# Two groups of eight tiles or four chains of four in a matrix normalisation, and a fourth weight pair in high and low parts

## The chip, the cores and the metric

The kernel runs on one core of one Trainium2 chip. The metric is the time of one execution on the device in microseconds (us), the median of three runs. An engine is named as in the profile: PE is the matrix engine (PEld its weight loads), DVE the vector engine, ACT the scalar engine, POOL the GpSimd engine, SP the engine that issues most DMA transfers (SPq its queue).

## The reference, cut to what matters

Eight samples of 256 tokens, 1024 features, float32. Each sample chooses one of 16 dense weights and one of 8 low-rank adapters. Cut to what is computed:

```python
# part one
h = einsum('bij,bkj->bik', x, L0_weight[ids1])      # a 1024 x 1024 weight per sample
h = layernorm(h) * gamma + beta
h = quant(h) @ quant(w1).T + b1                     # int8 fake-quant, scale per row
h = gelu(h)
h = quant(h) @ quant(w3).T + b3
x1 = x + h
# part two
c = x1 @ base_w.T + bias + scale * (x1 @ A[ids2].T) @ B[ids2].T
n = c / rms(c)
Hres = sinkhorn_log(n @ W_res.T + base)             # 4 x 4 per token, 50 iterations
Hpre, Hpost = softmax(n @ W_pre.T + ..), softmax(n @ W_post.T + ..)
Hres = (1 - g) * I + g * Hres                       # g = sigmoid(gate)
s = c as 4 streams of 256
out = x1 + Hres @ s + Hpost * ((Hpre . s) @ W_branch)
```

## The kernel before, in words

The tokens are 16 tiles of 128, two to a sample. The order of each engine's instructions is written out by hand: every engine has its own program (`step_a`, `step_b` and a tail, one version of each per engine), and semaphores tie them together. Nothing is reordered, so what waits on an engine holds up all that is written behind it.

**Part one** (0 to 398 us) has a `step_a(s)` for each sample s. PE's order in one is: transposes and product with w3 for the tiles of sample s-2, the transposes and product with w1 for sample s-1, and between them the four pairs `l0(s, 0..3)` of the gathered weight, a pair being two of the eight 128-row pieces. The products are L1087, the transposes L1019. A pair is computed in one of two ways. As it was loaded (L1010, `w_raw` times `x_raw`, float32), or in parts (L998): ACT rounds weight and x to high parts in the type fp32r (L731, L732), DVE subtracts these from the values to get low parts (L1546 for x, L1547 for the weight), and PE does high times high, low times high, and high times low. `parted(s, pr)` says which pairs are done so: pairs 0 to 2 of samples 3 to 6 (`FIRST = 3`). The high and low halves have no buffers of their own: `w_high(pr)` lies in `w_lo[pr]`, the x parts in `w_lo[3]`, and the four `w_hi` and `w_lo` are free until the base weight of part two is split into them (`split_hi`, ACT L616; low parts by DVE), which happens in the steps of samples 6 and 7. The work between two products of one tile is: ACT evacuates `hbuf` (L633), takes the sum of squares (L642), DVE centres and scales it, ACT rounds it (L652), PE transposes it, ACT evacuates `qT` (L672); after w1 DVE scales (L1461), ACT does the gelu (L657) and rounds again (L661, `quant2`); after w3 DVE writes `x1buf` (L1488).

In the same stretch rows for part two are prepared: the low parts of the adapter rows and of the heads' rows, written to the scratch tensor `stack_low_scratch` by SP. Four stores count `all_st` up to 64: two in the step of sample 2, two (`store_head_rows`, L358 and L359) in that of sample 6 (`step_a_base`). `heads_in` and `bias_in`, from which the last two go, lie in the memory of the `w_hi` buffers. So ACT waits for `all_st` before `split_hi(3)`.

**Part two** (398 to 621 us) has a `step_b(b)` per sample: base weight in high and low parts (L1204, three quarters of the step), the adapter, the heads, the softmaxes, the branch input. A product of the adapter or the heads is L1192; it stands once a step on the chain. In steps 0 to 3 DVE has idle stretches ahead of `xT_lo` (L1539), the low part of the transposed tiles.

**The Sinkhorn normalisation** is done on the factors: DVE alternates row and column factors `ka`, `kb`, each by a product (L1725), a sum (L1729) and a reciprocal (L1732); 49 iterations run in this loop, and the start (L1691 to L1716, `sinkhorn_start`) and the finish (L1746 to L1755) do the rest. The 16 tiles are two groups of 8, and each group two chains of 4 tiles whose instructions alternate, 12 an iteration. Group 0 is started after step 3, and its iterations stand in the steps of samples 4 to 7 as 11, 12, 13 and 13 (`B_ITERS`); group 1 is started after the last softmax, and all its iterations follow it.

**The tail** (621 to 749 us): while DVE iterates group 1, ACT and PE mix the first eight tiles. For one tile ACT builds `post` (L927, four instructions) and `blk` (L935, sixteen) from the 4 x 4 matrices, PE adds the rest and the branch (L1310, L1316) and `blk` times the streams (L1325), and ACT evacuates (L942). `select(g)` (L1339) and `pick(g)` (DVE L1787, L1794) bring the matrices of a group into the form `hs` that the blocks need. The rest and branch of the last eight tiles are done there too, ahead of their matrices (`AHEAD = 4` of them first, four at the end), and then PE has only `blk` times streams left (L1356), with blocks by DVE (L1821) and three by ACT (`BY_ACT`), and DVE adds (L1835). Before it `keep_warm` runs 48 transposes (L1366) while the last three iterations go on.

## Time and profile before

| | |
|---|---|
| median of three runs | 749.83 us (749.0, 749.83, 750.52) |
| the profiled execution, its own time | 751.13 us |
| its span, first to last instruction | 749.3 us |
| PE busy | 707.8 us, 94% |
| DVE busy | 526.2 us, 70% |
| ACT busy | 397.3 us, 53% |
| POOL busy | 79.9 us, 11% |
| mean granted clock of PE | 0.977 of full |
| chain of waits, share by engine | PE 74%, DVE 19%, ACT 5%, issue 2%, DMA 1% |

The span in 40 slices of 18.7 us. A digit is the busy share in tenths, 9 for 90% or more; PEclk is the clock granted to PE:

```profile
PE   8999999999999999999998999999999993999957
DVE  4569676979742976776663341428899998999985
ACT  1255846666741584828355443444534432899614
PEclk9999999999999999999998999999999996999979
```

PE is the bound until about 717 us; then DVE alone works until the last factors are there, and after it PE and DVE finish the last eight tiles.

### The profile page before, as it was taken

The page shows a single profiled execution, that of the slowest core. Times are in us where ns is not written, and L with a number is a line of the kernel's source. Part 1 is how long each engine was busy: PE and PEld are TensorE (multiplying, and loading weights), DVE is VectorE, ACT ScalarE, POOL GpSimd, SP SyncE. Part 2 cuts the span into 40 slices and gives each one's busy share as a digit, 9 for nine tenths or more (in the row PEclk, how much of TensorE's full clock was granted, in tenths as well). Part 3 has the DMA queues.
Part 4 walks back from the last instruction along what each step waited for, and adds up shares of the span by engine and source line. Part 5 has one row for each costly group of instructions (what it writes and reads, how often), then busy time and mean ns, then how long its engine had stood idle before and what let it go on. Part 6 is the DMA issues. An engine that isn't in the chain of part 4 may idle for free.

```text
span 749.3 us, 10394 instructions
## 1 busy us (share of the span) xinstructions
PE 707.8 (94%) x3292; PEld 477.6 (64%) x3292; DVE 526.2 (70%) x1869; ACT 397.3 (53%) x714; POOL 79.9 (11%) x57
## 2 busy tenths in 40 slices
PE   8999999999999999999998999999999993999957
PEld 5444445656536565445656888887888872677656
DVE  4569676979742976776663341428899998999985
ACT  1255846666741584828355443444534432899614
POOL 0201400302030032732040000000000000000000
PEclk9999999999999999999998999999999996999979
DMA  7997255558734236851232303303123086847106
GB/s 297 409 410 284 94 196 207 187 165 300 294 111 169 101 126 197 327 199 64 69 127 74 127 13 115 127 0 128 56 74 128 0 281 224 262 162 244 64 1 224
DMA packets 52477, 124.35 MB, mean 166 GB/s; under 512 B 6211, under 2 KB 31939, under 8 KB 46920
## 3 DMA queue, kind: packets, MB, share of 16 engines
q1 hardware_dynamic: 51128, 120.96, 45.6%
q10 hardware_dynamic: 1296, 2.74, 1.0%
q8 instruction: 26, 0.43, 0.2%
q14 instruction: 27, 0.22, 0.1%
HBM read 97.96 MB, written 25.72 MB: 165 GB/s over the span
## 4 chain that ended last, share of the span: by engine, by line
PE 74%; DVE 19%; ACT 5%; issue 2%; DMA 1%; SPq 0%; ACTq 0%; DVEq 0%
PE PS L1204 20%; PE PS L1010 18%; PE PS L1087 13%; PE PS L998 8%; DVE kprod L1725 4%; DVE ksum L1729 4%; PE PS L1192 2%; PE PS L1019 2%; DVE ka L1732 2%; DVE kb L1732 2%; PE PS L1356 2%; PE PS L1121 2%; PE PS L1178 2%; PE PS L1238 1%; PE PS L1366 1%
## 5 line engine op out<-in xcount | busy, mean ns | idle before, releaser
L1010 PE MATMUL PS<-w_raw,x_raw 128*128 128x512 f32 x320 | 141.7, 596 | 1.3 <-DMA w_raw<-cond_w_dram 0.9
L1010 PEld LDWEIGHTS PS<-w_raw,x_raw 128*128 128x128 f32 x320 | 59.4, 190 | 69.6 <-issue 69.6
L1204 PE MATMUL PS<-w_hi,xT_hi 128*128 128x512 f32 x256 | 103.0, 402 | 0.0
L1204 PE MATMUL PS<-w_hi,xT_lo 128*128 128x512 f32 x256 | 100.5, 393 | 0.0
L1204 PE MATMUL PS<-w_lo,xT_hi 128*128 128x512 f32 x256 | 100.4, 392 | 0.0
L1539 DVE TENSOR_TENSOR xT_lo<-PS,xT_hi 128x512 fp32r<-128x512 f32 x32 | 20.5, 682 | 66.0 <-ACT xT_hi L753 66.0
L1729 DVE TENSOR_REDUCE ksum<-kprod 128x16 f32<-128x64 f32 x392 | 66.3, 211 | 0.0
L577 POOL TENSOR_TENSOR xres<-xres,vecs 128x1024 f32<-128x1024 f32 x16 | 42.5, 2680 | 218.1 <-DMA xres<-x_tok_dram 218.1
L672 ACT ACTIVATE qT<-PS,round_c 128x1024 bf16<-128x1024 f16 x32 | 35.4, 1108 | 56.6 <-PE PS L1019 56.6
L1087 PE MATMUL PS<-w3q,qT 128*128 128x512 bf16 x256 | 57.8, 379 | 1.0 <-ACT qT L672 1.0
L1087 PE MATMUL PS<-w1q,qT 128*128 128x512 bf16 x256 | 57.9, 379 | 0.3 <-ACT qT L672 0.3
L1204 PEld LDWEIGHTS PS<-w_hi,xT_lo 128*128 128x128 f32 x256 | 48.3, 189 | 10.4
L1204 PEld LDWEIGHTS PS<-w_lo,xT_hi 128*128 128x128 f32 x256 | 48.5, 190 | 9.2
L1204 PEld LDWEIGHTS PS<-w_hi,xT_hi 128*128 128x128 f32 x256 | 48.6, 190 | 9.1
L833 ACT ACTIVATE y<-PS 128x512 f32<-128x512 f32 x32 | 18.0, 592 | 57.0 <-PE PS L1212 57.0
L1087 PEld LDWEIGHTS PS<-w1q,qT 128*128 128x128 bf16 x256 | 24.5, 98 | 32.6 <-issue 5.5
L1087 PEld LDWEIGHTS PS<-w3q,qT 128*128 128x128 bf16 x256 | 24.2, 98 | 33.2 <-issue 4.4
L1461 DVE SCALAR_TENSOR_TENSOR gbuf<-PS,lnst,vecs 128x512 f32<-128x512 f32 x32 | 23.5, 748 | 30.9 <-PE PS L1087 30.8
L998 PE MATMUL PS<-w_lo 128*128 128x512 f32 x96 | 38.6, 402 | 1.2 <-DVE w_low L1547 1.0
L998 PE MATMUL PS<-w_lo,x_low 128*128 128x512 f32 x96 | 38.0, 395 | 0.0
L998 PE MATMUL PS<-w_low,w_lo 128*128 128x512 f32 x96 | 37.8, 394 | 0.0
L1488 DVE SCALAR_TENSOR_TENSOR x1buf<-PS,q2st,vecs 128x512 f32<-128x512 f32 x32 | 23.0, 746 | 19.1 <-PE PS L1087 19.1
(209 smaller groups left out, 1358.0 us busy)
## 6 DMA issues: line engine op xcount, KB each, us to landing
w_raw<-cond_w_dram SPq DMA_DIRECT2D x31, 1024.0 KB, 5.4
x_raw<-x_tr_dram SPq DMA_DIRECT2D x32, 256.0 KB, 6.7
stage<-w_dram SPq DMA_DIRECT2D x16, 512.0 KB, 16.2
xres<-x_tok_dram SPq DMA_DIRECT2D x8, 1024.0 KB, 8.2
x_scratch<-x1buf SPq DMA_DIRECT2D x16, 512.0 KB, 6.7
x1n<-x_scratch SPq DMA_DIRECT2D x16, 512.0 KB, 6.6
y_scratch<-y SPq DMA_DIRECT2D x16, 512.0 KB, 3.7
stage<-base_w_nat_dram SPq DMA_DIRECT2D x8, 512.0 KB, 8.7
```

Of the source, the lines that this page charges most:

```text
L577: nc.gpsimd.tensor_tensor(xres[:, t, :], xres[:, t, :], vecs[:, V_B3, :], ALU.add).then_inc(xb3_done, 1)
L672: nc.scalar.activation(qT[t][:, :, :], PS[:, T_BANK + t, :].bitcast(F16).rearrange("p (c n) -> p c n", c=KC), ACT.Identity, bias=round_c[: ...
L998: mm = pe.matmul(PS[:, 2 * t + h, :], xx[:, c, t * P:(t + 1) * P], ws[:, c, h * H2:(h + 1) * H2], start=(pr == 0 and c == 0 and xx is xh a ...
L1010: mm = pe.matmul(PS[:, 2 * t + h, :], x_raw[pr][:, c, t * P:(t + 1) * P], w_raw[pr][:, c, h * H2:(h + 1) * H2], start=(pr == 0 and c == 0) ...
L1087: mm = pe.matmul(PS[:, O_BANK + h, :], qT[t][:, c, :], wq[:, c, h * H2:(h + 1) * H2], start=(c == 0), stop=(c == KC - 1))
L1204: pe.matmul(PS[:, 2 * t + h, :], xx[:, c, t * P:(t + 1) * P], ws[c // 2][:, c % 2, h * H2:(h + 1) * H2], start=(c == 0 and xx is xT_hi and ...
L1461: nc.vector.scalar_tensor_tensor(out=g[:, h * H2:(h + 1) * H2], in0=PS[:, O_BANK + h, :], scalar=lnst[:, t, 8:9], in1=vecs[:, V_SW1, h * H ...
L1488: nc.vector.scalar_tensor_tensor(out=x1buf[t][:, h * H2:(h + 1) * H2], in0=PS[:, O_BANK + h, :], scalar=q2st[:, t, 1:2], in1=vecs[:, V_SW3 ...
L1539: nc.vector.tensor_tensor(xT_lo[:, 4 * h:4 * h + 4, t * P:(t + 1) * P], PS[:, T_BANK + h, :].rearrange("p (c n) -> p c n", c=4), xT_hi[:, ...
L1725: nc.vector.tensor_tensor(kprod[i][:, :, :, :], (kmat if row else kmat_t)[i][:, :, :, :], cols(v, HG), ALU.mult).then_inc(k_step[i], 1)
L1729: nc.vector.tensor_reduce(ksum[i][:, :, :], kprod[i][:, :, :, :], AX.X, ALU.add).then_inc(k_step[i], 1)
L1732: nc.vector.reciprocal(new[i][:, :, :], ksum[i][:, :, :]).then_inc(k_step[i], 1)
```

## The change

Of part one:

- Pair 3 is also done in parts, for samples 4, 5 and 6 (`FIRST = (3, 3, 3, 4)`). Its high weight part goes to `w_hi[3]`. ACT rounds it ahead of pairs 0 and 1 of the next sample, DVE takes its low part in the same place.
- `heads_in` and `bias_in` lie two places lower (`2 * PAIRS - 4`), in the memory of `w_hi[2]`. So ACT's wait for `all_st` stands before `split_hi(2)`, and SP issues `store_head_rows` one transfer earlier, ahead of `load_base(3)`.
- Two transfers `load_nat(6)` and `load_nat(7)` of the step of sample 4 go behind the loads of weight pair 3. The semaphores `ln_mean` and `ln_var` are one, `ln_stat`.

Of part two and the tail:

- The Sinkhorn work is four chains of four tiles. `sinkhorn_start` does one chain, in steps 2, 4 and 6 and after the last softmax. The shares of iterations per step are in `SHARES`: chain 0 alone in steps 2 and 3, chains 0 and 1 together in 4 and 5, four iterations of them and the finish of chain 0 in step 6, then chains 1 and 2.
- After the last softmax: chain 3 is started; 6 iterations of chains 1 and 3, finish of 1, 33 iterations of chains 2 and 3 (with `pick_first` after two and `lo_xp` after eight), finish of 2, then chain 3 alone: 3 iterations, `pick(2)`, 1, two mixing blocks, 6, finish.
- Twelve tiles are mixed as eight were before (`MIXED`), the blocks of the last two of these by DVE; four tiles are left for the end (`LAST`), one of their blocks by ACT. `AHEAD` is 2, `BLK` 5. `select` and `pick` come in three: for tiles 0 to 7, 8 to 11 and 12 to 15. `keep_warm` runs 24 transposes during the last two iterations.
- The finish of a chain uses the product that the loop left in `kprod` for the last column factor; the one that was made anew is gone.

The first place: SP's queue in the step of sample 6, before and after. `w_raw<-cond_w_dram` is the load of sample 7's weight pair 1, which waits until DVE has read the buffer.

Before:

```order
L314 TENSOR_LOAD ids
L314 ISA x2
L320 ISA [waits wlo_done]
L320 DMA w_raw<-cond_w_dram 128x2048
L310 DMA x_raw<-x_tr_dram 128x512
L325 DMA w_raw<-base_w_dram 128x2048 [waits l0_pair]
L358 DMA stack_low_scratch<-heads_in 128x24 [waits all_low]
L359 DMA stack_low_scratch<-bias_in 1x24
```
After, the same stretch:

```order
L327 TENSOR_LOAD ids
L327 ISA x2
L333 ISA [waits wlo_done]
L333 DMA w_raw<-cond_w_dram 128x2048
L323 DMA x_raw<-x_tr_dram 128x512
L371 DMA stack_low_scratch<-heads_in 128x24 [waits all_low]
L372 DMA stack_low_scratch<-bias_in 1x24
L338 DMA w_raw<-base_w_dram 128x2048 [waits l0_pair]
```
The two stores now stand one transfer earlier, ahead of the base weight's piece 3, and still behind the weight load that waits for `wlo_done`.

The second place: ACT in the steps of samples 6 and 7, with the semaphores an instruction waits for. L616 and L631 are `split_hi`; the first one shown is `split_hi(2)`. What follows it is the gelu (L657, L672) and quant2 (L661, L676) of tile 1 of sample 5.

Before:

```order
L642 ACTIVATE x1buf,lnst<-hbuf,lnst 128x1024 [waits x1_st0,ln_mean]
L616 ACTIVATE w_hi<-w_raw 128x2048 [waits wld2]
L657 ACTIVATE gbuf<-gbuf 128x1024 [waits g_pre]
L648 ACT_TABLE_LOAD
L648 ACTIVATE lnst<-lnst 128x1 [waits ln_step]
L661 ACTIVATE gbuf<-gbuf,round_c,q2st 128x1024 [waits g_step]
L639 ACTIVATE lnst<-lnst 128x1 [waits l0_evac]
L642 ACTIVATE x1buf,lnst<-hbuf,lnst 128x1024 [waits x1_st1,ln_mean]
L652 ACTIVATE hbuf<-hbuf,round_c,lnst 128x1024 [waits ln_step]
L672 ACTIVATE qT<-PS,round_c 128x1024 [waits t3_done,m1_done]
L616 ACTIVATE w_hi<-w_raw 128x2048 [waits all_st,wld3]
```
After:

```order
L657 ACTIVATE x1buf,lnst<-hbuf,lnst 128x1024 [waits x1_st0,ln_stat]
L631 ACTIVATE w_hi<-w_raw 128x2048 [waits all_st,wld2]
L672 ACTIVATE gbuf<-gbuf 128x1024 [waits g_pre]
L663 ACT_TABLE_LOAD
L663 ACTIVATE lnst<-lnst 128x1 [waits ln_step]
L676 ACTIVATE gbuf<-gbuf,round_c,q2st 128x1024 [waits g_step]
L654 ACTIVATE lnst<-lnst 128x1 [waits l0_evac]
L657 ACTIVATE x1buf,lnst<-hbuf,lnst 128x1024 [waits x1_st1,ln_stat]
L667 ACTIVATE hbuf<-hbuf,round_c,lnst 128x1024 [waits ln_step]
L687 ACTIVATE qT<-PS,round_c 128x1024 [waits t3_done,m1_done]
L631 ACTIVATE w_hi<-w_raw 128x2048 [waits wld3]
```
The wait for `all_st` has moved nine instructions up, from the split of piece 3 to that of piece 2, so that the gelu and quant2 of that tile now stand behind it.

The third place: DVE in the step of sample 5, with buffer numbers. `x1buf1` is the end of sample 3's tile 1, `gbuf0` the scaling after w1 of sample 4's tile 0.

Before:

```order
L1493 TENSOR_TENSOR x1buf1<-x1buf1,xres 128x1024
L1546 TENSOR_TENSOR x_low0<-x_raw0,w_lo3 128x512
L1547 TENSOR_TENSOR w_low0<-w_raw0,w_lo0 128x2048
L1546 TENSOR_TENSOR x_low1<-x_raw1,w_lo3 128x512
L1547 TENSOR_TENSOR w_low1<-w_raw1,w_lo1 128x2048
L1461 SCALAR_TENSOR_TENSOR gbuf0<-PS,lnst,vecs 128x512 x2
L1465 TENSOR_TENSOR gbuf0<-gbuf0,vecs 128x1024
```
After:

```order
L1542 TENSOR_TENSOR x1buf1<-x1buf1,xres 128x1024
L1595 TENSOR_TENSOR x_low3<-x_raw3,w_lo3 128x512
L1596 TENSOR_TENSOR w_low3<-w_raw3,w_hi3 128x2048
L1595 TENSOR_TENSOR x_low0<-x_raw0,w_lo3 128x512
L1596 TENSOR_TENSOR w_low0<-w_raw0,w_lo0 128x2048
L1595 TENSOR_TENSOR x_low1<-x_raw1,w_lo3 128x512
L1596 TENSOR_TENSOR w_low1<-w_raw1,w_lo1 128x2048
L1510 SCALAR_TENSOR_TENSOR gbuf0<-PS,lnst,vecs 128x512 x2
```
One more pair of low parts stands ahead of the two that were there, and `gbuf0` behind all three.

The fourth place: the end of PE's program. L1310 and L1335 add the rest, L1316 and L1341 the branch, L1325 and L1353 the mixing, L1339 and L1379 are `select`, L1366 and L1406 `keep_warm`.

Before, from the mixing of tile 7 on, up to the first of the last eight tiles:

```order
L1325 MATMUL PS<-my3,blk1 128x256 x4
L1310 MATMUL PS<-nr4,ident 128x512 x2
L1316 MATMUL PS<-br,post0 128x256 x4
L1310 MATMUL PS<-nr5,ident 128x512 x2
L1316 MATMUL PS<-br,post1 128x256 x4
L1310 MATMUL PS<-nr6,ident 128x512 x2
L1316 MATMUL PS<-br,post0 128x256 x4
L1310 MATMUL PS<-nr7,ident 128x512 x2
L1316 MATMUL PS<-br,post1 128x256 x4
L1366 MATMUL PS<-ident 128x128 x48
L1339 MATMUL PS<-hres1,sel 128x128 x4
L1356 MATMUL PS<-ny0,my0 128x256 x4
```
After, the same end begins:

```order
L1335 MATMUL PS<-nr2,ident 128x512 x2
L1341 MATMUL PS<-br,post0 128x256 x4
L1335 MATMUL PS<-nr3,ident 128x512 x2
L1341 MATMUL PS<-br,post1 128x256 x4
L1379 MATMUL PS<-hres1,sel 128x64 x4
L1335 MATMUL PS<-mr0,ident 128x512 x2
L1341 MATMUL PS<-br,post0 128x256 x4
L1353 MATMUL PS<-my0,blk3 128x256 x4
```
and ends:

```order
L1335 MATMUL PS<-mr3,ident 128x512 x2
L1341 MATMUL PS<-br,post1 128x256 x4
L1353 MATMUL PS<-my3,blk1 128x256 x4
L1406 MATMUL PS<-ident 128x128 x24
L1379 MATMUL PS<-hres1,sel 128x64 x4
L1396 MATMUL PS<-ny0,my0 128x256 x4
```
Four tiles that PE mixed after the last select now go before it, behind a select of their own, and two rest-only tiles are behind the eighth instead of four.

The diff, cut to its core:

```diff
-    FIRST = 3
+    FIRST = (3, 3, 3, 4)
-    BLK = 3
-    BY_ACT = (5, 6, 7)
-    AHEAD = 4
+    BLK = 5
+    CHAINS = NT // HG
+    LAST = HG
+    MIXED = NT - LAST
+    BY_ACT = (LAST - 1,)
+    BY_DVE = (MIXED - 2, MIXED - 1)
+    AHEAD = 2
...
         def parted(s, pr):
-            return FIRST <= s < GUEST and pr < PAIRS - 1
+            return FIRST[pr] <= s < GUEST
...
         def w_high(pr):
-            return w_lo[pr]
+            return w_hi[pr] if pr == PAIRS - 1 else w_lo[pr]
...
-        B_ITERS = (11, 12, 13, 13)
-        WARM_ITERS, WARM_LAST = 3, 48
+        STARTS = {2: 0, 4: 1, 6: 2}
+        SHARES = {2: (2, 3, 3, 3), 3: (3, 3, 2, 3), 4: (2, 3, 3, 3), 5: (3, 3, 3, 3), 7: (3, 3, 4, 0)}
+        FIRST_REST, SECOND_SHARES = 4, (3, 3)
+        WARM_ITERS, WARM_LAST = 2, 24
...
                 load_w(s + 1, 1)
+                store_head_rows()
                 load_base(3)
-                store_head_rows()
...
             def split_hi(pr):
                 act.wait_ge(wld[pr], pair_loads(GUEST - 1, pr) + 16)
-                if pr == PAIRS - 1:
+                if pr == PAIRS - 2:
                     act.wait_ge(all_st, 64)
...
                 evac_T(s - 1, 0, 1)
+                if s < GUEST:
+                    pair_high(s, 3)
                 pair_high(s + 1, 0)
...
                 finish_w3(s - 2, 1)
+                if s < GUEST:
+                    pair_low(s, 3)
                 pair_low(s + 1, 0)
...
             def step_b(b, first=False, last=False):
                 def share(i):
+                    if b in SHARES:
+                        iterations(SHARES[b][i], *((0,) if b < 4 else (0, 1) if b < 6 else (1, 2)))
+                    elif b == NB - 2 and i == 0:
+                        iterations(FIRST_REST, 0, 1)
+                        sinkhorn_finish(0)
+                    elif b == NB - 2 and i >= 2:
+                        iterations(SECOND_SHARES[i - 2], 1, 2)
                 lo_stacks(b)
                 if not first:
                     lo_xp(b - 1)
+                if b in STARTS:
+                    sinkhorn_start(STARTS[b], nothing)
                 share(0)
...
-            sinkhorn_start(1)
+            sinkhorn_start(3, beside_last_start)
             gather_next(NB - 1, 3)
-            iterations(1, 0, 2)
-            pick(0)
-            iterations(1, 2, 8)
+            iterations(SINKHORN - 1 - done[1], 1, 3)
+            sinkhorn_finish(1)
+            iterations(2, 2, 3)
+            pick_first()
+            iterations(6, 2, 3)
             lo_xp(NB - 1)
-            iterations(1, 10, SINKHORN - 11)
-            sinkhorn_finish(1)
+            iterations(SINKHORN - 1 - done[2], 2, 3)
+            sinkhorn_finish(2)
+            iterations(3, 3)
+            pick(2)
+            iterations(1, 3)
+            dve.wait_ge(hs_step, 4)
+            for k in BY_DVE:
+                mix_block(k)
+            iterations(SINKHORN - 1 - done[3], 3)
+            sinkhorn_finish(3)
...
-            select(0)
-            for i in range(AHEAD):
...
+            rest_only(0, 0)
+            branch_transposes(NB - 1)
+            rest_only(1, 1)
+            select_first()
+            mix(0)
+            branch(NB - 1)
+            for k in range(1, GROUP):
+                mix(k)
+            rest_only(AHEAD + GROUP, 2)
+            rest_only(AHEAD + GROUP + 1, 3)
+            select(2)
+            for k in range(GROUP, MIXED):
+                mix(k)
             keep_warm()
-            select(1)
-            for i in range(GROUP):
+            select(3)
+            for i in range(LAST):
                 last(i)
```

## Rows read from the trace of the kernel before

**Rows 1.** The chain of waits, steps 3 to 7: start, length, piece.
```profile
475.95 2.87 PE PS L1192 x24
...
537.47 2.87 PE PS L1192 x24
...
567.41 2.87 PE PS L1192 x24
...
578.08 5.48 PE PS L1204 x24
...
609.41 5.48 PE PS L1204 x24
```

**Rows 2.** The chain of waits, the last eight tiles.
```profile
728.65 14.05 PE PS L1356 x56
```

**Rows 3.** The chain of waits, steps of samples 3 to 5.
```profile
166.96 5.61 PE PS L998 x24
...
195.53 6.92 PE PS L1010 x16
```

**Rows 4.** Timeline of ACT, step of sample 6: start, length, instruction, [idle, releaser].
```profile
307.17 1.90 ACT L616 ACTIVATE w_hi<-w_raw 128x2048 fp32r<-128x2048 f32 x1
...
311.69 1.24 ACT L661 ACTIVATE gbuf<-gbuf,round_c,q2st 128x1024 f32<-128x1024 f32 x1 [0.16 <-DVE q2st L1476]
```

**Rows 5.** Timeline of DVE, step of sample 5.
```profile
254.49 0.69 DVE L1546 TENSOR_TENSOR x_low<-x_raw,w_lo 128x512 fp32r<-128x512 f32 x1
...
257.29 1.40 DVE L1461 SCALAR_TENSOR_TENSOR gbuf<-PS,lnst,vecs 128x512 f32<-128x512 f32 x2
```

**Rows 6.** Timeline of PE, steps of samples 6 and 7.
```profile
265.10 0.47 PE L998 MATMUL PS<-w_lo 128*128 128x512 f32 x1 [0.22 <-ACT hbuf L633]
...
314.90 0.61 PE L1019 MATMUL PS<-ident,gbuf 128*128 128x128 f16 x8
```

**Rows 7.** Timeline of SP's queue, the store of the bias row of the heads.
```profile
309.58 0.32 SPq L359 DMA_DIRECT2D stack_low_scratch<-bias_in  x1
```

**Rows 8.** The tile stack_low_scratch: all its DMAs, from issue to landing.
```profile
DMA to landing us min/median/max: 2.2/3.5/3.8
```

**Rows 9.** Timeline of DVE, steps of samples 3 and 4.
```profile
494.07 1.29 DVE L1539 TENSOR_TENSOR xT_lo<-PS,xT_hi 128x512 fp32r<-128x512 f32 x2 [12.85 <-ACT xT_hi L753]
...
508.95 0.29 DVE L1691 TENSOR_REDUCE ska<-zall 128x32 f32<-128x128 f32 x1
...
514.60 0.09 DVE L1716 MEMSET kb<- 128x16 f32 x2
```

**Rows 10.** Timeline of DVE, from the last softmax to the last factor.
```profile
623.34 0.17 DVE L1595 TENSOR_SCALAR hd<-hd 128x2 f32<-128x2 f32 x1 [1.13 <-ACT sq L837]
...
634.23 0.28 DVE L1691 TENSOR_REDUCE ska<-zall 128x32 f32<-128x128 f32 x1
...
640.85 0.35 DVE L1725 TENSOR_TENSOR kprod<-kmat,kb 128x64 f32<-128x64 f32 x2
...
644.10 0.69 DVE L1787 TENSOR_TENSOR hsr<-PS,mask_r 128x256 f32<-128x256 f32 x2
...
723.00 0.29 DVE L1753 TENSOR_SCALAR hres<-hres,gate_c 128x128 f32<-128x128 f32 x1
723.33 0.26 DVE L1755 TENSOR_SCALAR hres<-hres,gate_c 128x32 f32<-128x32 f32 x1
```

**Rows 11.** Timeline of ACT, one tile of the mixing.
```profile
672.75 1.40 ACT L927 ACTIVATE post<-ident,hp 128x128 f32<-128x128 f32 x4
673.93 3.51 ACT L935 ACTIVATE blk<-mask,hs 128x32 f32<-128x32 f32 x16
```

**Rows 12.** Busy time by stretch: us, busy us (instructions) of each engine, PEclk granted.
```profile
650.00:694.00 44.00, 42.87 (x170) 30.96 (x169) 44.00 (x323) 44.00 (x170) 0.00 (x0) 1.00 0.68 221
...
717.00:719.00 2.00, 1.43 (x7) 1.46 (x8) 2.00 (x17) 0.00 (x0) 0.00 (x0) 0.50 0.04 8
...
723.00:725.00 2.00, 2.00 (x20) 2.00 (x19) 0.55 (x2) 0.00 (x0) 0.00 (x0) 1.00 0.00 0
```

407 lines of the change are left out of this document (216 added, 191 removed).

## The prediction

> **What bounds the kernel now.** I read the slices first: PE is at nine tenths until about 717 us, then DVE works alone for some eight microseconds, then PE and DVE finish together. The chain of waits says which stretch belongs to whom. In part one and part two it is PE nearly throughout, so only what shortens PE's work, or what makes PE wait, counts there. A normal `step_b` takes 29.94 us (537.47 to 567.41); steps 3 and 4 together take 61.52, so 1.64 is lost to a late feeder, and between steps 6 and 7 it is 31.33, 1.39 lost [rows 1]. In the tail DVE's Sinkhorn iterations are the chain while ACT and PE mix, and then eight tiles follow in 749.3 - 728.65 = 20.65 us [rows 2]. So I worked out three sums: samples 4 to 6 of part one, the steps of part two, the tail. All times are on the clock of the profiled execution (751.13 us of its own time around a span of 749.3); it lies 1.3 us above the median, which I take off at the end.
>
> **Part one, the fourth pair.** A pair in parts takes 5.61 us on PE against 6.92 [rows 3], so three pairs give back 3 x 1.31 = 3.9 us if their parts are ready. What this adds: for each pair ACT rounds a weight and an x (1.90 us and less, the row of `w_hi` [rows 4]), about 2.3 us, and DVE takes the low parts, which for one pair need 257.29 - 254.49 = 2.80 us [rows 5]. They are ahead of the low parts of the next sample's pairs and of the scaling behind w1.
>
> In sample 4's step PE keeps about 0.9 of 1.31. In sample 5's step DVE comes to `gbuf0` 2.8 later. That has to pass gelu, quant2 and the transposes before PE can go on, and the feeders have no room: PE's first product of `l0(6, 0)`, at 265.10, waited 0.22 us for an evacuation by ACT already [rows 6]. So `l0(6, 0)` starts 2.8 - 0.9 = 1.9 later than before, and the gain of samples 4 and 5 is gone. Sample 6's pair gives 1.3, which brings PE to +0.6.
>
> **Part one, the wait that moved.** `split_hi(2)` started on ACT at 307.17 [rows 4]. Now it waits for all four stores. SP issued the last one at 309.58 with a start some 0.5 earlier [rows 7]; it is one transfer earlier now, but it stays behind the weight load that waits for DVE's low part, and the transfer that it passed needs no wait at that time, so I leave it at 309.1. Stores to this tensor take 2.2 us at least, 3.5 in the median and 3.8 at most to land [rows 8]: 309.1 + 3.5 = 312.6, and ACT starts the split 5.4 us later. Behind it, on the same engine, are the gelu and quant2 of sample 5's tile 1; quant2 ended at 311.69 + 1.24 = 312.93, 5.76 after the start of the split, so now at 318.35. PE's transposes of that tile (314.90 [rows 6]) come after sample 7's first pair and would be reached, after the gain of 1.3, at 313.6. Delay over before: 318.35 - 314.90 = 3.4, and the 1.9 shift of the whole stretch comes on top, since the store hangs on DVE's work that has shifted as well: **+5.3 us** for part one. With a landing of 2.2 it is 4.0, with 3.8 it is 5.6, and if the store has landed by the time that ACT asks, +0.6.
>
> **Part two.** Starting chains 0 and 1 earlier puts iterations into idle time that DVE has in steps 1 to 3 (12.85 us ahead of `xT_lo` [rows 9]). A start for 8 tiles took 514.60 + 0.09 - 508.95 = 5.75 us [rows 9]; most of it is latency, so I take 4.9 for 4 tiles. There are three such starts in steps now. In step 4: the start 4.9, and five iterations of two chains at 1.625 (3.25 for two [rows 10]: 640.85 to 644.10) is 8.1, and about 3.2 is carried in from step 3's last share; 12.85 of room leaves 3.1 late. The rest of the step's room takes that back but for 2.0, which PE sees at the transposes of the branch input in step 5. Before, the same place lost 1.64. In step 6 the start, four iterations and a finish give some 1.45 to PE, against 1.39 before step 7. Sum: 3.45 against 3.03, **+0.4 us**, between -1.1 and +1.9: below, if the starts hide entirely in steps that DVE had idle; above, if both starts reach PE with an iteration more.
>
> **The tail.** The last softmax begins at 623.34 [rows 10]; it comes 0.4 later by part two, and two `post` blocks of 1.18 (672.75 to 673.93 [rows 11]) now stand on ACT ahead of it, of which I take half of one, 0.6 (none to 2.4): +1.0. Four iterations and a finish that stood between softmax and start are gone, so the start of chain 3 is at 624.3 + 3.2 = 627.5 instead of 634.23, 6.7 earlier. Then on DVE: start to first iteration 5.7 (6.6 before, 634.23 to 640.85, for eight tiles); 6 + 33 iterations of two chains, 39 x 1.625 = 63.4; two finishes 1.4; `pick_first` 1.3; `lo_xp` 0.6; three single iterations.
>
> What is a single iteration? No row of before has it. It is six dependent instructions. Two independent ones take 0.35 (`kprod`, x2), a dependent one begins 0.04 after the other's end (723.00 + 0.29, 723.33) [rows 10]. If only the length counted, with 0.22 each and 0.035 between, six are 1.52; the bounds are half of a pair's, 0.81, and a whole pair's, 1.625. I take 1.52, since an instruction of a chain that waits for the one before has nothing beside it. `pick(2)` adds 0.8: it is over at 627.5 + 5.7 + 63.4 + 1.4 + 1.3 + 0.6 + 4.6 + 0.8 = 705.3.
>
> The Trainium skill, page "VectorE: DVE Perf Modes", section "The DRAIN you can't avoid", says that the next instruction doesn't issue until the pipeline has emptied, and that a semaphore between two costs nothing beyond this. By that rule no time is lost to waiting on one's predecessor, and a chain alone would be half of a pair. The two independent `kprod`, which overlap in 0.35 us, don't agree with it (the same section lets an instruction that isn't held start earlier).
>
> From 705.3 on it is not DVE that binds. Four tiles are still to be mixed, and their blocks can't be built before `pick(2)`. In the stretch from 650 to 694 ACT is busy throughout and PE for 42.87 of 44.00 us, with 170 records of each, 21 instructions a tile on ACT (5.4 us) and 20 on PE (5.16) [rows 12]. ACT needs `post` and block for tile 8, 1.18 + 3.5 = 4.6, then 5.5 for tile 9, PE ends with it at 717.1; tiles 10 and 11 have blocks from DVE and go at PE's pace, 2 x 5.16: 727.4. Then `keep_warm`, 24 at 0.1 (20 in 2.00 [rows 12]) 2.6; select and wait 0.7; `pick(3)` 0.8; first block to PE 0.8; the last four tiles. Eight took 20.65; one costs at most 2.0 (14.05 for 56 records, eight a tile [rows 2]), and less once blocks are ahead, I take 1.73: 20.65 - 6.9 = 13.7. End: 746.0. PE waits 3.6 us before the first of the four tiles. In the row of 717 to 719, where PE was not fed, the granted clock is 0.50, and 1.00 again in that of 723 to 725 [rows 12]; I allow 1.5 for a stretch at the lower level (0 to 3). 747.5 against 749.3: **-1.8 us** for part two and the tail together, between -5.4 (a single iteration of 0.81, no cold stretch, part two at its lower end) and 0 (an iteration of 1.625, 3 us of cold clock). DVE alone would be through at 719, ten microseconds earlier: what the four chains save DVE, the mixing takes.
>
> **Sum.** +5.3 - 1.8 = +3.5, 754.6 on the profiled clock, 753.3 as a median. Within 0.2% (748.3 to 751.3) a measurement can't tell it from no change.
>
> **The rivals.**
>
> *The store is early enough.* If SP had room to issue it before ACT asks (DVE's low part of weight pair 1, on which it hangs, done 5 us sooner against ACT's own progress), part one is +0.6 and the whole -1.2, 748.6. For it speaks that ACT is delayed too by its extra rounding; against it, that the load it stands behind was waiting, and that the landing alone is 3.5 of the 5.4.
>
> *DVE sets the end.* If mixing a tile took 2.6 us instead of 5.2, DVE would be done with chain 3 at 719 and the last four tiles would end at 735 or 736: 13.8 less in the tail, and with +5.3 about 741. For it speaks that DVE is the chain of the tail now; against it, ACT at 44.00 of 44.00.
>
> *A chain alone costs half of a pair.* If a dependent instruction starts no later than an independent one, a single iteration is 1.625 / 2 = 0.81, three are 2.1 less, and all behind them comes 2.1 earlier: 751.2. Against it speak the two `kprod` in 0.35. The rule of the Trainium skill that was weighed above is this case.
>
> *The steps slip (slower).* The three starts are dependent chains with ACT in them. The place is step 4 or 6, where DVE's carried work, the start and the iterations exceed the room by 3.1 in my sum; once it is beyond what the rest of the step takes back, each microsecond is one of PE. A start that found no room at all is 4.9, less the 2.0 counted: 756.2, and 757 to 758 with 3 us of cold clock.
>
> **How the numbers follow.** Forecast 0.42 (749.5 to 756.5: from the landing, the single iteration, the clock; a fifth of it within 0.2%). Store early 0.26, half faster. DVE at the end 0.12, faster. A chain alone at half 0.06, two thirds of it within 0.2%, the rest faster. Steps slip 0.14, slower. Faster 0.13 + 0.12 + 0.02 = 0.27, within 0.2% 0.08 + 0.13 + 0.04 = 0.25, slower 0.34 + 0.14 = 0.48. The range from 745.5 to 757 leaves out the second rival and the far end of the last; the forecast's own range is 749.5 to 756.5.
>
> **What would show it.** Right: pair 3 of samples 4 to 6 at 5.6 us on PE; `l0(6, 0)` some 1.9 later than 265.1 with PE idle before it; ACT idle about 5 us before its third `w_hi`, released by the DMA of `stack_low_scratch`, and PE idle before the transposes L1044 of sample 5's tile 1; the start of chain 3 near 627.5 plus the shift of part one; single iterations of 1.5; PE idle before tile 8, the last mix ending 22 us after `pick(2)`; DVE idle about ten before `pick(3)`. Wrong: the third `w_hi` not waiting for a DMA (first rival), DVE busy up to `pick(3)` and PE waiting for it (second), PE idle by more than 2.5 us at the branch transposes of steps 5 or 7 (the last). If all of part one's steps keep their 3.9 us, the forecast fails by nine.

## The result and the profile after

The changed kernel takes **761.84 us** (761.01 to 763.12, four runs); the kernel before took 750.17 on the same chip (749.0 to 751.2). The ratio is 1.016, 95% interval 1.014 to 1.018: slower, and by more than the range allowed (745.5 to 757.0). Its profiled execution has a time of 761.01 of its own around a span of 759.2; from its page, the chain of waits:

```profile
PE 66%; DVE 21%; ACT 8%; issue 2%; DMA 1%; POOL 1%; SPq 0%; ACTq 0%; DVEq 0%
```
The busy times are close to those of before (PE 705.5 us, DVE 552.1, ACT 410.2, POOL 82.8); POOL's share of the chain and DMA's, 1% each, are small and yet the story. The medians are 11.7 us apart and these two spans 9.9, since the profiled execution of before is among its slow ones and this one is the fastest of the four. To see where the 9.9 us are, I cut both executions at two places that they share: PE's transposes at the start of sample 5's step, near 220 us, and the first instruction of `step_b` of step 0 (L1192 before, L1217 now). Sample 4's own fourth pair (195.53 in [rows 3]) lies ahead of the first cut.

| us | up to the cut | from the cut to step 0 | from step 0 on | span |
|---|---|---|---|---|
| before | 220.63 | 177.76 | 350.91 | 749.3 |
| after | 219.10 | 190.73 | 349.37 | 759.2 |
| difference | -1.53 | **+12.97** | -1.54 | +9.9 |
| forecast | -0.9 | +6.2 | -1.8 | +3.5 |

The forecast's +5.3 for part one is split here: 0.9 gained by sample 4's pair, and 6.2 lost behind it. Of the 1.53 gained, 0.64 is there already at transposes ahead of that pair, which the change hardly reaches (126.76 before, 126.12 now), and is taken for chance. The other 0.9 is the pair, as forecast: 5.59 us on PE in the chain of waits, against 6.92, with 0.28 of waiting ahead of it.

```profile
126.76 0.61 PE L1019 MATMUL PS<-ident,gbuf 128*128 128x128 f16 x8
126.12 0.61 PE L1044 MATMUL PS<-ident,gbuf 128*128 128x128 f16 x8
194.70 0.62 PE L1044 MATMUL PS<-ident,hbuf 128*128 128x128 f16 x8 [0.28 <-ACT hbuf L667]
195.32 5.59 PE PS L1023 x24
```
(the first line is of before, the last of the chain of waits)

The loss is in part one: 409.83 - 398.39 + 0.64 = 12.1 us of it from the transposes at 126 on, against 5.3 forecast. The chain of waits shows the place (start, duration, what, and its line), to be held against [rows 4, 6, 7]:

```profile
305.39 5.39 POOL w_lo L586
312.30 5.35 DMA stack_low_scratch<-bias_in
317.73 1.91 ACT w_hi L631
319.64 0.96 ACT gbuf L672
320.62 1.23 DVE q2st L1520
322.26 1.25 ACT gbuf L676
323.56 1.03 PE PS L1044 x8
324.59 9.31 PE PS L1035 x16
```
One line is followed by the next: POOL's low weight part frees the buffer that SP's load waits for, behind which the stores stand; they are reported 5.35 us after the issue of the last one; ACT's third split, gelu, quant2; PE's transposes. They stood at 314.90 [rows 6], and are 8.66 later, 10.2 measured from the common cut and 9.3 from the transposes at 126. Then the pair that took 6.92 [rows 3] takes 9.31. The idle times and the wait of each in the list of instructions (in brackets what ended the idle time before it):

```profile
306.45 7.10 PE L1035 MATMUL PS<-w_raw,x_raw 128*128 128x512 f32 x16 [1.67 <-ACT hbuf L648]
317.73 1.91 ACT L631 ACTIVATE w_hi<-w_raw 128x2048 fp32r<-128x2048 f32 x1 [8.05 <-DMA stack_low_scratch<-bias_in]
323.56 1.03 PE L1044 MATMUL PS<-ident,gbuf 128*128 128x128 f16 x8 [6.55 <-ACT gbuf L676]
```
ACT had asked at 317.73 - 8.05 = 309.68. In the windows (stretch, length, then busy time and count of PE, PEld, DVE, ACT and POOL, then granted clock, DMA share, GB/s) the gap is followed by a stretch at the lower of TensorE's two levels:

```profile
317.00:323.50 6.50, 0.01 (x1) 0.00 (x0) 2.67 (x8) 5.58 (x6) 3.78 (x1) 0.66 0.37 152
323.50:328.00 4.50, 4.44 (x13) 2.38 (x14) 4.40 (x6) 2.34 (x5) 4.50 (x3) 0.50 0.56 204
328.00:331.00 3.00, 3.00 (x7) 1.34 (x6) 2.97 (x4) 3.00 (x3) 1.83 (x1) 0.79 0.33 131
```
PE was empty for 6.5 us, and then worked at 0.50 (1.2 GHz) until 328 and partly at it until 331: 9.31 - 6.92 = 2.4 us on top of the wait. So 10.2 + 2.4 make 12.6 of the 12.97.

From step 0 on the sum is near the forecast, but not by its terms alone (see the part on the prediction). In the rows of PE below, L1217 opens `step_b` of steps 5 and 6: 546.01 to 577.93 is 31.92 us against the 29.94 of [rows 1], 1.98 lost (2.0 forecast, the 1.58 at the branch transposes is its largest piece), while the 1.64 of before's step 4 is gone.

```profile
546.01 1.12 PE L1217 MATMUL PS<-xT_hi,av_hi 128*128 128x256 f32 x8
550.62 0.83 PE L1253 MATMUL PS<-ident,xp 128*128 128x128 f32 x4 [1.58 <-DVE xp L1688]
577.93 0.76 PE L1217 MATMUL PS<-xT_hi,av_hi 128*128 128x256 f32 x5
```
DVE in the tail, against [rows 10]: the start of chain 3, `pick(2)`, the end of the last six single iterations, and `pick(3)`:

```profile
637.53 0.22 DVE L1741 TENSOR_REDUCE ska<-zall 128x16 f32<-128x64 f32 x1
716.82 0.42 DVE L1851 TENSOR_TENSOR hsr<-PS,mask_r 128x256 f32<-128x256 f32 x1 [2.21 <-PE PS L1379]
729.83 0.27 DVE L1791 TENSOR_TENSOR hres<-kprod,kb 128x64 f32<-128x64 f32 x1
743.78 0.43 DVE L1851 TENSOR_TENSOR hsr<-PS,mask_r 128x256 f32<-128x256 f32 x1 [13.12 <-PE PS L1379]
```

| from the start of chain 3, us | forecast | measured |
|---|---|---|
| `pick_first` over | 20.7 | 20.74 |
| `pick(2)` over | 77.8 | 80.2 |
| last mix over (740.12 for `keep_warm`) | 99.9 | 102.6 |
| end of the span | 120.0 | 121.7 |

Six iterations of one chain, from the end of the two blocks to the finish, take 729.83 - 720.31 = 9.52, 1.59 each (1.52 forecast); DVE stands idle 13.12 before `pick(3)`.

### The profile page after: what moved, and what is told of

It reads as the page before. It is cut to its first block, busy times and chain, and to the rows that moved or that the text cites. A ratio compares the mean times of both kernels' runs of the same rounds, so it can differ in the third digit from the quotient of the medians.

```text
span 759.2 us, 10451 instructions
## 1 busy us (share of the span) xinstructions
PE 705.5 (93%) x3300; PEld 477.9 (63%) x3300; DVE 552.1 (73%) x1888; ACT 410.2 (54%) x730; POOL 82.8 (11%) x57
## 4 chain that ended last, share of the span: by engine, by line
PE 66%; DVE 21%; ACT 8%; issue 2%; DMA 1%; POOL 1%; SPq 0%; ACTq 0%; DVEq 0%
PE PS L1035 15%; PE PS L1229 12%; PE PS L1112 11%; PE PS L1023 8%; DVE kprod L1769 3%; DVE ksum L1773 3%; PE PS L1335 3%; PE PS L1341 3%; PE PS L1353 3%; PE PS L1044 2%; PE PS L1146 2%; DVE ka L1776 2%; DVE kb L1776 2%; DVE xp L1688 2%; PE PS L1217 1%
## 5 line engine op out<-in xcount | busy, mean ns | idle before, releaser
L1035 PE MATMUL PS<-w_raw,x_raw 128*128 128x512 f32 x272 | 122.9, 605 | 2.5 <-ACT hbuf L648 2.1
L1229 PE MATMUL PS<-w_lo,xT_hi 128*128 128x512 f32 x256 | 99.9, 390 | 0.0
L1035 PEld LDWEIGHTS PS<-w_raw,x_raw 128*128 128x128 f32 x272 | 51.5, 194 | 62.5 <-issue 60.6
L1773 DVE TENSOR_REDUCE ksum<-kprod 128x16 f32<-128x64 f32 x392 | 69.6, 212 | 2.2
L1229 PEld LDWEIGHTS PS<-w_hi,xT_lo 128*128 128x128 f32 x256 | 48.0, 188 | 10.3
L1023 PE MATMUL PS<-w_low,w_lo 128*128 128x512 f32 x120 | 47.4, 395 | 0.0
L1776 DVE RECIPROCAL ka<-ksum 128x16 f32<-128x16 f32 x196 | 38.5, 231 | 1.1
L1776 DVE RECIPROCAL kb<-ksum 128x16 f32<-128x16 f32 x196 | 38.4, 231 | 1.1
```

What stands on the lines that cost most here:

```text
L1023: mm = pe.matmul(PS[:, 2 * t + h, :], xx[:, c, t * P:(t + 1) * P], ws[:, c, h * H2:(h + 1) * H2], start=(pr == 0 and c == 0 and xx is xh a ...
L1035: mm = pe.matmul(PS[:, 2 * t + h, :], x_raw[pr][:, c, t * P:(t + 1) * P], w_raw[pr][:, c, h * H2:(h + 1) * H2], start=(pr == 0 and c == 0) ...
L1229: pe.matmul(PS[:, 2 * t + h, :], xx[:, c, t * P:(t + 1) * P], ws[c // 2][:, c % 2, h * H2:(h + 1) * H2], start=(c == 0 and xx is xT_hi and ...
L1773: nc.vector.tensor_reduce(ksum[c][:, :, :], kprod[c][:, :, :, :], AX.X, ALU.add).then_inc(k_step[c], 1)
L1776: nc.vector.reciprocal(new[c][:, :, :], ksum[c][:, :, :]).then_inc(k_step[c], 1)
```

## The experiments

Two theories stood against each other at first, and both turned out to hold: A has the larger part, and B takes what the pairs give. A, the wait: the loss is the store that ACT waits for, and what PE's gap costs in clock. B, the pair: the fourth pair in parts makes its feeders late and would lose without any wait. I give each run's ratio to the kernel before with its interval, and its length from the first cut to step 0 ("stage", 177.76 before, 190.73 after) and from there to the end ("rest", 350.91 and 349.37). Both are of one execution each. The rest of the same instructions varies: as before it is 350.9, 349.0 (e3) and 348.4 (h12), as changed 349.4, 348.5 (e1) and 345.2 (e2). The stage varies by stretches at the lower clock: one near 230, while PE is busy throughout, is in e2, e4, g8 and h12 alone and costs each 1.4 to 1.6 us, and a like one behind the wait at 265 is in e1, e3 and g5.

### Which half loses

**e2_tail_only**: part one as before.

```diff
-    FIRST = (3, 3, 3, 4)
+    FIRST = (3, 3, 3, GUEST)
-            for i in range(2 * PAIRS - 4):
+            for i in range(2 * PAIRS - 2):
-                if pr == PAIRS - 2:
+                if pr == PAIRS - 1:
                     act.wait_ge(all_st, 64)
```
(SP's order of `load_nat`, `load_base(3)` and the stores is as before too)

> The changed kernel with part one as before: pair 3 of all samples as loaded, the heads' rows in their old place, the wait at the split of piece 3. Theory (all of the loss is in part one, +11.4 us there, and -1.5 in part two and the tail): 748.5 to 751.5. Rival (part of the loss is in the four chains): 754 or more.

748.68 us, 0.999 (0.998 to 1.001); stage 179.3 (1.5 of it a stretch at the lower clock that before has not), rest 345.2. **e3_pairs_only**: the kernel before with part one of the changed one.

> The kernel before with part one as changed (pair 3 in parts, heads' rows lower, wait at the split of piece 2, one statistics semaphore), part two and tail as before. Theory: 750.0 + 11.4 = 760 to 762.5. Rival (the two parts disturb each other): under 757.

762.17 us, 1.019 (1.017 to 1.021); stage 190.2. The two together account for the result: part one costs all of it, the four chains are worth nothing that can be told.

### The wait

**h12_wait_only**: the kernel before, with nothing but the memory of the heads' rows, the stores' place and ACT's wait moved.

```diff
-        for i in range(2 * PAIRS - 2):
+        for i in range(2 * PAIRS - 4):
-                if pr == PAIRS - 1:
+                if pr == PAIRS - 2:
                     act.wait_ge(all_st, 64)
-                load_base(3)
                 store_head_rows()
+                load_base(3)
```


> The kernel before with the wait alone moved: heads' rows in the memory of piece 2, all_st waited for at the split of piece 2, the stores one transfer earlier; no fourth pair, tail as before. Theory: ACT asks at 307.2, the store goes out at 309.1 and lands after 5.4 (as measured after the change), so quant2 ends at 320.2 and PE's transposes come at 320.2 instead of 314.9, +5.3, and up to 2.4 for the clock behind the gap: 754.5 to 757.5. Rival (the wait hurts only together with the fourth pair): under 751.5.

757.66 us, 1.011 (1.009 to 1.013), 0.2 above what the theory expected and far from the rival. The stage is 186.72 - 177.76 = 8.96 us longer. 1.5 of it is a stretch at the lower clock that has nothing to do with the wait (from 229 to 233 the granted clock is 0.57, and PE is busy all the time); the wait alone, with no fourth pair, costs the other 7.4: PE's transposes come 6.0 later, and they and the pair behind them are slower by 0.4 and 1.0.

```profile
310.31 0.32 SPq L359 DMA_DIRECT2D stack_low_scratch<-bias_in  x1
316.30 1.91 ACT L616 ACTIVATE w_hi<-w_raw 128x2048 fp32r<-128x2048 f32 x1 [7.79 <-DMA stack_low_scratch<-bias_in]
322.12 1.03 PE L1019 MATMUL PS<-ident,gbuf 128*128 128x128 f16 x8 [5.81 <-ACT gbuf L661]
```
The last store was issued at 310.31 and ACT went on at 316.30, 6.0 later.

**e1_store_early**: the changed kernel, the store ahead of the weight load.

```diff
-                load_w(s + 1, 1)
                 store_head_rows()
+                load_w(s + 1, 1)
```


> The changed kernel with the two stores of the heads' rows one load earlier still on SP, ahead of the load of weight pair 1 of sample 7 that waits for POOL. Theory (the moved wait): the stores go out about 303 instead of 312.3 and have landed before ACT asks at 309.7, so ACT's 8.05 us of idle, PE's 6.55 and the 2.4 us of the slow pair behind it are gone: 761.8 - 9 = 752.5 to 754. Rival (the fourth pair's own work on ACT, DVE and POOL costs the time, the wait only shows it): the next feeder is late instead, 758 or more.

753.65 us, 1.008 (1.006 to 1.011); stage 183.41. The first row is the last store, issued 2.2 us after the transfer ahead of the two (301.13):

```profile
303.35 0.45 SPq L372 DMA_DIRECT2D stack_low_scratch<-bias_in  x1
313.78 1.91 ACT L631 ACTIVATE w_hi<-w_raw 128x2048 fp32r<-128x2048 f32 x1 [3.60 <-DMA stack_low_scratch<-bias_in]
```
The time is as the theory expected, but the stores had not landed when ACT asked. Issued nine microseconds sooner, they were reported only 3.9 sooner: 10.4 us after the issue of the last, behind five transfers issued between 299 and 302. In the trace their own packets (96 bytes each) move between 311.4 and 313.1: the time passes ahead of them. **m1_store_by_act**: the same stores from ACT's own queue.

```diff
+                    act.wait_ge(all_low, 4)
+                    nc.scalar.dma_start(low_dram[0:NB * RANK, D:D + NH], heads_in[:, :]).then_inc(all_st, 16)
+                    nc.scalar.dma_start(low_dram[NB * RANK:NB * RANK + 1, D:D + NH], bias_in[:, :]).then_inc(all_st, 16)
```
(behind `split_hi(1)`; SP's two are gone)

> The changed kernel with the two stores of the heads' rows issued by ACT, behind its split of piece 1 (about 305.5), instead of by SP. Theory (on SP's queue they stood behind the weight load and behind 3 MB of transfers): they land by 309.5, ACT hardly waits, PE's 6.55 us and the slow pair go: ratio 1.004 to 1.007, 752.5 to 755. Rival (the stretch's traffic delays any store): they land after 311, ratio over 1.009.

752.16 us, 1.003 (1.001 to 1.005); stage 181.65.

```profile
303.20 0.60 ACTq L800 DMA_DIRECT2D stack_low_scratch<-bias_in  x1
311.12 1.91 ACT L630 ACTIVATE w_hi<-w_raw 128x2048 fp32r<-128x2048 f32 x1 [1.10 <-DMA stack_low_scratch<-bias_in]
```
A little faster than expected, though the stores land at 311.0 and not by 309.5. At the same time of issue as e1's it took 7.9 us instead of 10.4: 2.5 belong to SP's queue, the rest is there from an empty queue too, while the large loads are in flight. It is not chance: g5, g6 and k16 below, with e1's place of the stores, have 10.3 each, m2 and m3, with m1's, 7.3 each. The Trainium skill, page "DMA: Bandwidth & Descriptors", section "Queues, rings and completion order", says that each DMA engine takes turns between the queues, a packet at a time, and that a semaphore's increment lands only after every earlier write of that engine, whatever queue it is from; the row of ACT's queue agrees with it.

**e4_gap_filled** puts 48 transposes into PE's gap, to tell the clock's part from the wait's.

```diff
+                if s == NB - 3 and t == 1 and which == 3:
+                    for i in range(FILL):
+                        pe.transpose(PS[:, T_BANK + t, (i % 4) * P:(i % 4 + 1) * P], ident[:, :], ident[:, :])
```


> The changed kernel with 48 transposes of the identity on PE in the gap of 6.55 us, ahead of the late transposes; the wait itself stays. Theory (the pair behind the gap took 9.31 instead of 6.92 us because the granted clock had fallen): the wait stays and the 2.4 us go, 759 to 760. Rival (the pair is slow for another reason, its data or its banks): 761.8, unchanged.

760.37 us, 1.015 (1.013 to 1.018); stage 189.8. The transposes behind the gap (the 48 put in take 5.40), the pair in the chain of waits, then two windows with columns as above:

```profile
325.54 0.62 PE L1045 MATMUL PS<-ident,gbuf 128*128 128x128 f16 x8 [1.61 <-ACT gbuf L677]
326.16 6.92 PE PS L1036 x16
```
```profile
228.00:232.00 4.00, 4.00 (x21) 3.29 (x20) 0.36 (x1) 1.45 (x2) 0.00 (x0) 0.58 0.59 240
323.50:328.00 4.50, 2.89 (x17) 1.66 (x16) 4.25 (x9) 3.15 (x6) 4.50 (x2) 1.00 0.18 31
```
The clock stays at 1.00 and the pair takes 6.92, as it did before the change, instead of 9.31: the rival is out. The stage is only 0.9 shorter than that of the changed kernel, because this execution has the stretch near 230 (granted clock 0.58, where the changed kernel's has 1.00), which makes all behind it 1.5 later. Without it the gap filled would give back 2.4 to 2.5 of the stage, the 2.4 of the pair. In the medians it is 1.5.

### The pair without the wait

**g5_split_late**: e1, and the split with its wait behind quant2.

```diff
-                if s == GUEST - 1:
-                    split_hi(2)
                 gelu(s - 1, 1)
                 ln_root(s, 0)
                 quant2(s - 1, 1)
+                if s == GUEST - 1:
+                    split_hi(2)
```


> The changed kernel with the stores ahead of the weight load (as in the first experiment) and, on ACT, the split of piece 2 moved behind quant2 of sample 5's tile 1. Theory (in the first experiment the store still took 10.4 us to land, ACT waited 3.60 and PE 2.10 for what stands behind the split): nothing stands behind it now, PE's 2.1 us go: 753.65 - 2.1 = 751.5. Rival (the later split makes the load of weight pair 2 of sample 7 late instead, which waits for POOL's low part): 753 to 755.

754.42 us, 1.006 (1.004 to 1.008), in the rival's range; stage 183.26, +5.5 though nothing that PE needs stands behind the store any longer. 1.5 of this is the stretch at the lower clock from 266 to 269, right behind a wait. PE around sample 6's first pair:

```profile
265.85 1.04 PE L1044 MATMUL PS<-ident,gbuf 128*128 128x128 f16 x8 [2.22 <-ACT gbuf L676]
266.94 0.76 PE L1023 MATMUL PS<-w_lo 128*128 128x512 f32 x1
```
**g6_skip_sample5**: g5 with pair 3 in parts for samples 4 and 6 only.

```diff
-            return FIRST[pr] <= s < GUEST
+            return FIRST[pr] <= s < GUEST and not (pr == PAIRS - 1 and s == 5)
```


> As the one before, and pair 3 in parts only for samples 4 and 6, not for 5. Theory (the low parts of sample 5's pair, 2.8 us of DVE ahead of the scaling, are what makes the first pair of sample 6 late; the pair itself gives 1.31): 1.5 less than the one before, about 750.0. Rival (something else, as ACT's rounding, makes it late): 1.3 more than the one before, 752.8.

751.44 us, 1.003 (1.002 to 1.004); stage 180.07. Sample 5's pair costs 3.0 in the medians (3.2 in the stage, with the slow stretch that goes with its wait in g5). **k16_dve_order**: g5 with DVE's scaling in the step of sample 5 ahead of the low parts.

```diff
-                pair_low(s + 1, 0)
-                pair_low(s + 1, 1)
-                finish_w1(s - 1, 0)
+                scale_w1(s - 1, 0)
+                pair_low(s + 1, 0)
+                range_w1(s - 1, 0)
+                pair_low(s + 1, 1)
```


> As the fifth (stores early, split of piece 2 late, all three fourth pairs), and on DVE in sample 5's step the scaling of sample 4's tile 0 stands ahead of the low parts of pairs 0 and 1 of sample 6, its range between them. Theory (the low parts ahead of the scaling make PE wait 0.5 + 2.2 + 0.5 us before the first pair of sample 6): 2.8 to 3.2 less than 754.4, ratio 1.002. Rival (ACT's rounding or the loads are what is late): 1.006 as before.

752.96 us, 1.005 (1.003 to 1.007), only 1.5 less than g5 where 2.8 to 3.2 were expected; stage 179.97, of an execution 2.6 faster than the median (750.36).

```profile
263.55 0.47 PE L1023 MATMUL PS<-w_lo 128*128 128x512 f32 x1
304.36 1.96 PE L1035 MATMUL PS<-w_raw,x_raw 128*128 128x512 f32 x4 [1.67 <-ACT hbuf L648]
```
`l0(6, 0)` is reached at 263.55 with no wait ahead of it (266.94 in g5): that loss was the order on DVE, as the forecast had it. A later one remains, 1.67 before `l0(7, 0)`, the same as in the changed kernel. What made it stands in DVE's and POOL's rows of the changed kernel (no run removed it, so this is read from rows alone):

```profile
291.68 2.29 DVE L1596 TENSOR_TENSOR w_low<-w_raw,w_hi 128x2048 fp32r<-128x2048 f32 x1
292.29 6.13 POOL L586 TENSOR_TENSOR w_lo<-w_raw,w_hi 128x2048 fp32r<-128x2048 f32 x1 [18.34 <-ACT w_hi L631]
295.64 3.86 DVE L1514 TENSOR_TENSOR gbuf<-gbuf,vecs 128x1024 f32<-128x1024 f32 x1
305.39 5.38 POOL L586 TENSOR_TENSOR w_lo<-w_raw,w_hi 128x2048 fp32r<-128x2048 f32 x1 [6.97 <-ACT w_hi L631]
```
and in those of before at the same places:

```profile
288.34 1.23 DVE L1493 TENSOR_TENSOR x1buf<-x1buf,xres 128x1024 f32<-128x1024 f32 x1
290.14 4.52 POOL L571 TENSOR_TENSOR w_lo<-w_raw,w_hi 128x2048 fp32r<-128x2048 f32 x1 [14.12 <-ACT w_hi L616]
294.25 1.50 DVE L1465 TENSOR_TENSOR gbuf<-gbuf,vecs 128x1024 f32<-128x1024 f32 x1
```
POOL's instruction takes 4.52 when it starts with DVE out of the way. At 292.29 DVE was in `w_low` until 293.97: 1.68 + 4.5 = 6.2, and it took 6.13. DVE's addition, 1.23 for such operands, began at 295.64 while POOL was busy until 298.42, and ended 1.08 behind that, at 299.50. Before, it began at 294.25, POOL ended at 294.66 and it ended 1.09 behind. In these rows each waits until the other is wholly through. The Trainium skill, page "SBUF — State Buffer", section "SBUF: two separate sides", states this as a lock held for a whole instruction between GpSimd and a VectorE instruction with two SBUF inputs; the rows agree with it. So the low parts of sample 6's fourth pair, 2.80 of work added to DVE, lay across the start of POOL's instruction, and both came later: the addition that PE's feeders wait for took 2.4 longer, POOL's next low part 0.9 longer, and on that one hangs the store.

**m2_store_act_dve_order**: m1 with k16's order (both diffs above), and **m3_all_three**: that with the branch input early (g7 below).

> As the one before, with DVE's order in sample 5's step as in the earlier experiment (scaling ahead of the low parts of sample 6). Theory: another 2 to 3 us less, ratio 1.001 to 1.003. Rival: the gain is taken by the next late feeder (the evacuation before sample 7's first pair), no difference.

> As the one before, and lo_xp straight after pick_first in the tail. Theory (the fourth pair brings no more than its feeders cost): ratio 0.996 to 0.999, no better than the early branch without the fourth pair (0.994 and 0.996). Rival (with its stalls gone the fourth pair gives 3 us): under 0.994.

m2: 750.57 us, 1.002 (0.999 to 1.004), stage 178.59. m3: 747.42, 0.998 (0.996 to 0.999), stage 178.64. Both ratios are as expected; m2 is 1.6 below m1, a little less than the 2 to 3 of the theory. With both causes treated the stage is still 0.8 above that of before, where the two pairs in it should put it 2.6 below. What takes these 3.4 is in the rows of PE in m2: it waits 6.64 in the stage, 2.7 more than before, and 0.7 is small shifts.

```profile
254.82 0.50 PE L1025 MATMUL PS<-w_hi,w_lo 128*128 128x512 f32 x1 [0.41 <-DVE w_low L1598]
280.48 3.63 PE L1114 MATMUL PS<-w3q,qT 128*128 128x512 bf16 x16 [0.78 <-ACT qT L686]
305.27 7.10 PE L1037 MATMUL PS<-w_raw,x_raw 128*128 128x512 f32 x16 [1.67 <-ACT hbuf L647]
```
The first is in sample 5's own fourth pair, the last before `l0(7, 0)`. With the 0.9 that sample 4's pair keeps ahead of the cut, the three pairs come out at nothing: PE gives back 3.9, and the feeders take as much. Theory B holds beside A.

### The tail

**g7_branch_early**: e2, and DVE makes the branch input of sample 7 before the iterations. **k7_again** is the same kernel in another session.

```diff
             pick_first()
+            lo_xp(NB - 1)
             iterations(6, 2, 3)
-            lo_xp(NB - 1)
```


> The changed kernel with part one as before (tail and part two only), and the low part of the last branch input (lo_xp) straight after pick_first instead of 6 iterations later. Theory (in the tail PE and ACT with twelve tiles of mixing are the bound, and PE waits 3.66 us for lo_xp and runs slowly after it): 748.7 - 4 = 744 to 745.5. Rival (the chain of DVE's iterations sets the end): 748.7, unchanged.

> The kernel of the early branch once more, to see whether its 745.1 stands. Theory (PE's wait for lo_xp was worth what the medians said): ratio to before 0.992 to 0.995, as it was. Rival (most of it was the clock's state in those four runs, since in the profiles the mixing that was saved is waited for again at pick(2)): 0.996 to 0.999.

745.11 us, 0.994 (0.992 to 0.996), and 745.39, 0.996 (0.995 to 0.998): the fastest kernel of all, and faster than the one before in both sessions, though the second ratio lies in the range that k7's rival named. The wait of 3.66 that PE had there is gone. Yet in the profiled executions the rest is 345.6 and 345.4 against e2's 345.2: part of the time is waited again at `pick(2)` (PE 2.57 for ACT's `post` of tile 8, 0.66 in e2), and part of the gain in the medians (3.6) is that e2's runs spread from 745.3 to 750.2 and g7's first four did not (those of its repeat do, 745.2 to 750.3). How it divides stays open.

**g8_five_less**: e2 without five of the last single iterations, so that tiles 12 to 15 have fewer Sinkhorn iterations.

> Part one as before, tail as changed, with 5 of the last single iterations of chain 3 left out (tiles 12 to 15 get fewer normalisation steps). 5 x 1.59 = 8 us less work on DVE. Theory (DVE waits 13 us for PE there): 748.7, unchanged within 1 us. Rival (DVE's chain sets the end): 741.

748.42 us, 0.998 (0.996 to 1.000) against e2's 748.68.

```profile
731.18 0.42 DVE L1851 TENSOR_TENSOR hsr<-PS,mask_r 128x256 f32<-128x256 f32 x1 [21.11 <-PE PS L1379]
```
The eight microseconds taken from DVE came back as idle time, 21.11 instead of the 13.12 of e2 and of the changed kernel. DVE's last iterations are not what the end waits for.

**k13_pick2_early**: g7 with `pick(2)` after one single iteration instead of three.

```diff
-            iterations(3, 3)
+            iterations(1, 3)
             pick(2)
```


> The same with pick(2) after one single iteration of chain 3 instead of three. Theory (with the branch early, DVE's two single iterations of 1.59 us are what PE and ACT wait for between select(2) and the first of the four tiles): 2 to 3 us less than the one beside it. Rival (ACT and PE are not ready sooner): the same.

746.31 us, 0.996 (0.995 to 0.998): no gain over k7 beside it, as the rival had it.

**h9_blocks_by_dve**: g7, all four late mixing blocks built by DVE, `select(2)` ahead of the last two rest-only tiles.

```diff
-    BY_DVE = (MIXED - 2, MIXED - 1)
+    BY_DVE = (MIXED - 4, MIXED - 3, MIXED - 2, MIXED - 1)
```


> On the kernel of the early branch (part one as before, lo_xp straight after pick_first): the blocks of tiles 8 to 11 all by DVE, and select(2) ahead of the last two rest-only tiles on PE. Theory (PE is the bound of the tail and still waits 1.94 us for ACT's post and first block there): 745.1 - 2 to 3 = 742 to 743.5. Rival (DVE's chain is reached as the bound): 745.

749.28 us, 1.000 (0.999 to 1.001). The expectation failed: PE stood before `select(2)` for 2.54, waiting for the finish of chain 2, and 1.97 for a load. **h10_mix_early** keeps the blocks on DVE but leaves `select(2)` where it was, and picks chain 0 by itself so that mixing starts sooner; **h11_mix_early_pair4** adds pair 3 in parts for sample 4 alone.

```diff
-            iterations(SINKHORN - 1 - done[1], 1, 3)
-            sinkhorn_finish(1)
-            iterations(2, 2, 3)
-            pick_first()
+            pick(0)
+            iterations(2, 1, 3)
```


> As the early branch, blocks of tiles 8 to 11 by DVE, and a select and a pick of its own for chain 0 (finished in step 6), straight after the start of chain 3, so that the mixing of tiles 0 to 3 begins some 12 us sooner; chain 1's pick follows after tile 2. Theory (the mixing was the bound and started late; now it ends about when DVE's chain 3 does): 736 to 740. Rival (DVE's chain was close behind as a bound, 13 us of idle minus what moves): not under 743.

> As the one before, and pair 3 in parts for sample 4 alone (where nothing on ACT or DVE was late). Theory (that pair keeps 0.4 to 1.0 of its 1.31): 0.4 to 1.0 less than the one before. Rival (every fourth pair costs its feeders as much as it gives): the same or more.

747.41 us, 0.997 (0.995 to 0.998), and 747.31, 0.997 (0.996 to 0.998). h10's 736 to 740 failed by seven and more, and h11's pair gives nothing that can be told.

```profile
700.31 0.90 PE L1385 MATMUL PS<-hres,sel 128*128 128x64 f32 x3 [14.35 <-DVE hres L1806]
```
In h10 mixing begins 12 us sooner and PE then waits 14.35 us for chain 2. So PE and ACT bind the tail, and DVE's 39 double iterations stand close behind: taking work from one side alone only changes who waits.

## Why the prediction was wrong

**The step that failed is "Part one, the wait that moved".** Its mechanism held: ACT's third split waited for the stores, and PE for what stands behind it. Its size did not: part one lost 12.1 us against 5.3. In order, counted from the transposes at 126 (0.64 is added to each time of the changed kernel):

- The fourth pairs up to there were right. Sample 4's kept 0.9 of its 1.31 as forecast, and `l0(6, 0)` came at 266.38, 1.9 later than before, as forecast; k16 shows that the named cause, three low parts ahead of the scaling, is it.
- The time of issue. The prediction had 309.1, plus 1.9 of shift, 311.0; it was 312.30 + 0.64 = 312.9, 1.9 later. The prediction had SP's load wait for DVE's low part, and the text ahead of it says the same. It waits for POOL's (L571 before, L586 now), whose row ends at 310.78; SP issues the load at 310.96 and the last store at 312.30. POOL's instruction started late and was lengthened by DVE's.
- The landing: 5.35 against 3.5. This was a misreading: the times of [rows 8] are those of the eight loads `estage<-stack_low_scratch` from that tensor, made in part two, and no store is among them. In the same trace of before, the semaphore of the stores gets its last step at 318.04, 8.5 us after the issue of the last store at 309.58, and the split that waited for it then started half a microsecond later (the line below). In h12, e1 and m1 the same stores took 6.0, 10.4 and 7.9.
- Together 1.9 + 3.4 + 1.9 + 1.85 = 9.1 against the 9.3 measured at the transposes.
- The clock. No term stood for it in part one, though [rows 12] showed 0.50 behind a stretch in which PE was little fed, and the tail's sum had 1.5 for it. It cost 2.4 in the pair and 0.4 in the transposes (1.03 for 0.61).

```profile
318.58 1.90 ACT L616 ACTIVATE w_hi<-w_raw 128x2048 fp32r<-128x2048 f32 x1
```
Of the 6.8 us that the forecast lacked in part one, the issue is 1.9, the landing 1.85, the clock 2.8; 0.2 is unaccounted for. One more loss was foreseen by no term, PE's 1.67 before `l0(7, 0)`. It hides in this kernel behind the longer wait for the stores and shows in m1, m2 and k16.

**Part two was right where PE's row can be followed.** The 2.0 in step 5 was 1.98, the 1.64 of step 4 went. Chain 3 started at 637.5, or 626.1 without the 11.4 by which step 0 came later, against 627.5. Of the 1.4 that this is better, 1.1 is a flaw of the execution of before: its step 0 took 17.51 and its step 1 29.95, with a granted clock of 0.86 from 395 to 420, while the changed kernel has 15.51 and 30.85 at 1.00, and so have h12 and e3 (15.49 and 30.9), whose part two is that of before.

**The tail was right within two and a half microseconds.** From the start of chain 3 it took 121.7 here and 117.6 in e2, with the same instructions, against 120.0. That the rest came out at -1.54 against -1.8 is luck, as rests of the same instructions differ by more; in the medians e2 is 0.3 below the kernel before, in an interval that holds both nothing and the forecast. A single iteration is 1.59, near the 1.52 taken; "A chain alone costs half of a pair" (0.81) is false, and so is the rule of the Trainium skill, page "VectorE: DVE Perf Modes", section "The DRAIN you can't avoid", if read so that independent neighbours gain nothing: two chains take 1.625 together and one 1.59. `pick(2)` was 2.4 late, as PE's select came late to it (2.21); in e2 it was over after 77.8, as forecast. "DVE sets the end" is false by g8. "The store is early enough" is false for where the store stands; with the store out of the way (g5) the whole was still slower, by the fourth pairs. Its +0.6 held until sample 6's pair was through (0.7 on the clock from 126), and failed by the wait before `l0(7, 0)`. "The steps slip" did not happen.

"Slower" was the likeliest of the three. The upper end of the range, 757.0, leaned on a landing of 3.8 and on the steps slipping; a longer landing and the clock in part one were in no bound.

## What to carry to other kernels

Before a wait for a DMA is moved ahead of other work on an engine, take its landing from the same transfer in that very stretch, with the same transfers ahead of it in the queue, and look whether a row of times is of stores or of loads; a few bytes among large loads took 5 to 10 us here. Follow what the issuing queue's previous transfer waits for back to an instruction, and count what a gap on PE gives back at the lower clock. Ask of two executions at what clock each ran before their difference is read as a gain or a loss. Cheap work added to DVE is not priced by its length where POOL reads SBUF at the same time: look which instructions of the two would come to overlap.

## What the runs showed of the hardware

- Two small stores (128x24 and 1x24, one semaphore) were reported 5.35 us after the issue of the second in the changed kernel, 6.0 in h12, 10.4 in e1, 7.9 from ACT's queue in m1, and 8.5 in the kernel before, where the base weight's load stood ahead of them too.
- DVE and POOL excluded each other for whole instructions, each reading two operands from SBUF: 6.13 for 4.52 and 3.86 for 1.23, to within 0.15 of what waiting for the other's end gives.
- After 6.5 us without work on PE, the granted clock was 0.50 for 4.5 us and 0.79 for three more; a pair took 9.31 instead of 6.92. With 5.40 us of transposes in the gap it took 6.92, at 1.00.
- The clock fell in single executions without a gap of that kind: from 228 to 232 in e4 the granted clock was 0.58 with PE busy for all of the 4.00 us, and in the changed kernel 1.00. Such a stretch cost 1.4 to 1.6 us of the stage.
